# Edge counts of a graph layer: the first tile without registers, its tables built earlier, low halves of three weight pages moved

## What is computed

```python
e = leaky_relu(s_src[src] + s_dst[dst], 0.2)
emax = segment_max(e, dst, num_segments=n)
ee = exp(e - emax[dst])
denom = segment_sum(ee, dst, num_segments=n)
alpha = ee / denom[dst]
out = segment_sum(alpha[:, :, None] * h[src], dst, num_segments=n)
```

## Time and profile before

| | us |
|---|---|
| median of three runs | 1904.43 (1903.36 to 1904.77) |
| the profiled execution, own time | 1903.6 |
| its span, first to last instruction | 1901.9 |
| TensorE busy | 1851.5 |
| VectorE busy | 1296.5 |
| ScalarE busy | 654.5 |
| GpSimd busy | 558.1 |

### The profile page before, as it was taken

The page is one execution under the profiler, slowest core; times in us unless marked ns, Lnnn a source line. Parts: engine busy times, 40 slices in busy tenths (PEclk is TensorE's granted clock), DMA queues, the critical chain, the costliest instruction groups (busy, mean ns, idle before and its releaser), DMA issues.

```text
span 1901.9 us, 28584 instructions
## 1 busy us (share of the span) xinstructions
PE 1851.5 (97%) x10824; PEld 1758.4 (92%) x10824; DVE 1296.5 (68%) x2242; ACT 654.5 (34%) x1243; POOL 558.1 (29%) x441
## 2 busy tenths in 40 slices
PE   6999999999899999999999999999999999999998
PEld 4678999999899999989999999999999999999998
DVE  7987579998894323878796654454558966465548
ACT  6534238887884411225211111111341111211113
POOL 1000001210001132214355654444024455455420
PEclk9999999999999999999999999999999999999999
DMA  5433302122244210033311111111240111111314
GB/s 166 123 117 103 104 14 59 44 58 60 70 142 140 67 50 1 26 98 106 97 41 34 34 50 34 51 48 56 80 139 26 34 50 35 50 34 34 112 47 125
DMA packets 83133, 131.17 MB, mean 69 GB/s; under 512 B 7462, under 2 KB 53320, under 8 KB 82990
## 3 DMA queue, kind: packets, MB, share of 16 engines
q1 hardware_dynamic: 78430, 115.97, 20.8%
q10 hardware_dynamic: 4560, 13.31, 2.3%
HBM read 101.06 MB, written 28.20 MB: 68 GB/s over the span
## 4 chain that ended last, share of the span: by engine, by line
PE 86%; DVE 5%; ACT 5%; issue 3%; ACTq 0%; SPq 0%; DVEq 0%; DMA 0%
PE pb L809 20%; PE pa L809 17%; PE pb L1304 11%; PE pb L1284 9%; PE pa L870 5%; PE pb L1314 5%; PE pb L947 3%; PE pa L1029 3%; PE pb L1190 3%; PE pa L983 2%; PE pb L1029 2%; ACT sm L1787 1%; PE pb L817 1%; PE pb L1065 1%; ACT o1h L1813 1%
## 5 line engine op out<-in xcount | busy, mean ns | idle before, releaser
L809 PE MATMUL pa<-dw_hi,hh 128*125 128x384 f32 x608 | 156.8, 339 | 1.7 <-issue 1.1
L809 PE MATMUL pa<-dw_hi,hl 128*125 128x384 f32 x608 | 156.0, 338 | 0.0
L809 PE MATMUL pa<-dw_lo,hh 128*125 128x384 f32 x608 | 155.6, 337 | 0.0
L2713 DVE TENSOR_TENSOR hl<-tr,hh 128x448 fp32r<-128x448 f32 x144 | 152.1, 1056 | 5.0
L2711 DVE CAST hh<-tr 128x448 fp32r<-128x448 f32 x144 | 78.7, 546 | 88.2 <-ACT tr L2047 83.0
L2081 ACT ACTIVATE cp<-pb 128x448 f32<-128x448 f32 x32 | 17.4, 544 | 323.1 <-PE pb L1304 316.4
L2047 ACT ACTIVATE tr<-pb,V 128x448 f32<-128x448 f32 (+1 forms) x96 | 57.1, 597 | 198.7 <-PE pb L1284 142.1
L1492 POOL CAST dw_hi<-raw 128x768 fp32r<-128x768 f32 x48 | 49.2, 1025 | 230.7 <-PE pa L809 228.5
L870 PE MATMUL pa<-S1h,D1h 125*125 125x418 bf16 x510 | 103.4, 356 | 8.1 <-DVE S1h L2207 8.1
L809 PEld LDWEIGHTS pa<-dw_hi,hh 128*125 128x125 f32 x608 | 108.8, 185 | 2.2 <-issue 1.3
L809 PEld LDWEIGHTS pa<-dw_lo,hh 128*125 128x125 f32 x608 | 109.6, 185 | 0.0
(11 more groups left out here) (470 smaller groups left out, 5134.7 us busy)
## 6 DMA issues: line engine op xcount, KB each, us to landing
raw<-in_L_mix_fc_w SPq DMA_DIRECT2D x48, 384.0 KB, 3.4
raw<-in_L_ffn_w SPq DMA_DIRECT2D x47, 384.0 KB, 3.4
md<-md_d SPq DMA_DIRECT2D x11, 546.9 KB
md_d<-mds SPq DMA_DIRECT2D x10, 546.9 KB
raw<-in_L_mix_qkv_w SPq DMA_DIRECT2D x24, 192.0 KB, 4.2
md<-md_d ACTq DMA_DIRECT2D x8, 546.9 KB
TOK<-in_x SPq DMA_DIRECT2D x10, 336.0 KB
xn_d<-TOK SPq DMA_DIRECT2D x10, 336.0 KB
```

The lines of the kernel that those rows point to most:

```text
L809: last = nc.tensor.matmul(slot[:, c, :], x_[:, cols], w_[:, c * HD2:(c + 1) * HD2], start=(k == 0 and n == 0), stop=(k == len(blocks) - 1 ...
L2713: v.tensor_tensor(hb_lo[b][:, o:o + w], z, hb_hi[b][:, o:o + w].bitcast(fp32), ALU.subtract).then_inc(sem("h_lo"), 1)
```

## The change

The start of the first tile's rows is written as the constant 0, so that VectorE needs no register for its 16 fixed products and can begin once the limits `bc` are formed; `bc[0, 3]` is set to 85 by a `memset`, with one more chained wait. The copy to `bnd` moves behind the fourth product's tables, and the register for the loop count is loaded behind the sixteenth. On TensorE the three transposes of the small vectors move behind the sixth product, and the register loads for tile 0 and 1 behind the sixteenth. The low parts of the Wu pages, which stood as 0 and 1 before the loop and 2 behind tile 0, now stand as 0 behind tile 0, 1 behind tile 1 and 2 behind tile 2. Nothing changes on ScalarE, GpSimd and SP.

```diff
--- before.py
+++ after.py
@@ -242,7 +242,7 @@
                 kept[name] = (kind, before)
                 before += n
 
-        follow("pe_once", ("e_bb", 1), ("e_tr", 1), ("v_tr", 1), ("e_row", 1), ("tb0", 1), ("tb1", 1), ("r_log", 1), ("r_gb", 1))
+        follow("pe_once", ("e_bb", 1), ("e_tr", 1), ("e_row", 1), ("v_tr", 1), ("tb0", 1), ("tb1", 1), ("r_log", 1), ("r_gb", 1))
         follow("pe_rows", ("wt_mm", NT), ("g_mm", 2 * NT), ("kv_mm", 2 * NT), ("qg_mm", QJOBS), ("pj_mm", NT))
         follow("pe_side", ("c0_mm", 1), ("ssb_mm", 2 * NT), ("ssb2_mm", NT), ("xm_tr", NT), ("l_tr", NT), ("y_tr", NT))
         follow("pe_sums", ("e_acc", NT), ("at_o", STEPS), ("kvp", 2 * NT))
@@ -832,11 +832,13 @@
                     last = nc.tensor.transpose(pb[0:TP, 1, (2 * v + half) * EW:(2 * v + half) * EW + NEP],
                                                RM["ef"][:, v, half * TP:(half + 1) * TP], ident[0:NEP, 0:NEP])
             last.then_inc(sem("e_tr"), 1)
-            pe.wait_ge(*at("v_in", 16 * (len(VROWS) + len(VROWS2) + 1)))
-            vst = RM["t0_0"]
-            nc.tensor.transpose(pb[:, 0, 0:NV1], vst[0:NV1, 0:P], ident[0:NV1, 0:NV1])
-            nc.tensor.transpose(pb[:, 0, P:P + NV2], vst[0:NV2, P:2 * P], ident[0:NV2, 0:NV2])
-            nc.tensor.transpose(pb[0:C2, 0, 2 * P:2 * P + 2], vst[0:2, 2 * P:2 * P + C2], ident[0:2, 0:2]).then_inc(sem("v_tr"), 1)
+            def vector_transposes():
+                pe.wait_ge(*at("v_in", 16 * (len(VROWS) + len(VROWS2) + 1)))
+                vst = RM["t0_0"]
+                nc.tensor.transpose(pb[:, 0, 0:NV1], vst[0:NV1, 0:P], ident[0:NV1, 0:NV1])
+                nc.tensor.transpose(pb[:, 0, P:P + NV2], vst[0:NV2, P:2 * P], ident[0:NV2, 0:NV2])
+                nc.tensor.transpose(pb[0:C2, 0, 2 * P:2 * P + 2], vst[0:2, 2 * P:2 * P + C2], ident[0:2, 0:2]).then_inc(sem("v_tr"), 1)
+
             pe.wait_ge(*at("e_bc", 1))
             nc.tensor.matmul(pb[0:1, 3, 0:NT], RM["bc"][:, 0:1], ident[0:NT, 0:NT], start=True, stop=True)
             nc.tensor.matmul(pb[0:1, 3, 16:16 + NT], RM["bc"][:, 2:3], ident[0:NT, 0:NT], start=True, stop=True)
@@ -861,7 +863,7 @@
                     pe.wait_ge(*at("v_cp", 1))
                 if t >= 2:
                     pe.wait_ge(*at("e_sb", t - 1 if t <= XFIRST else t))
-                if t < XFIRST:
+                if 0 < t < XFIRST:
                     turns_of(t + 1)
                     turns_before(t + 1)
 
@@ -874,6 +876,13 @@
                 for n in range(2 * FIXED):
                     pe.wait_ge(*at(f"oh{n % RING}", fixed_use(turns, t, n)))
                     edge_products(n % RING, n == 0)
+                    if t == 0 and n == 5:
+                        vector_transposes()
+                if t == 0:
+                    pe.wait_ge(*at("bnd", 1))
+                    turns_of(0)
+                    turns_of(1)
+                    turns_before(1)
                 with pe.Fori(0, turns[t][0]) as p:
                     for q in range(2):
                         pe.wait_ge(*at(f"oh{q}", fixed_use(turns, t, 2 * FIXED + q) + p))
@@ -908,9 +917,7 @@
                     last = nc.tensor.matmul(pa[0:TP, 2 + c, 0:HD2], ones[:, 0:TP], RE["c0w"][:, c * HD2:(c + 1) * HD2], start=True, stop=True)
                 last.then_inc(sem("c0_mm"), 1)
 
-            pe.wait_ge(*at("bnd", 1))
             pe.wait_ge(*at("c_const", 3))
-            turns_of(0)
             for t in range(NT):
                 edge_counts(t)
                 for u in x_tiles(t):
@@ -2171,16 +2178,19 @@
             ch.link(v.tensor_scalar(bb[:, 0, :], pb[0:NT, 2, 0:NEP], bc[:, 7:8], None, ALU.is_lt))
             ch.link(v.scalar_tensor_tensor(out=bb[:, 1, :], in0=pb[0:NT, 2, P:P + NEP], scalar=bc[:, 6:7],
                                            in1=bb[:, 0, :], op0=ALU.is_ge, op1=ALU.mult))
-            v.tensor_tensor_reduce(out=bb[:, 3, :], in0=bb[:, 1, :], in1=ix[:, 1, :], scale=1.0, scalar=1.0,
-                                   op0=ALU.mult, op1=ALU.max, accum_out=bc[:, 3:4])
+            ch.link(v.tensor_tensor_reduce(out=bb[:, 3, :], in0=bb[:, 1, :], in1=ix[:, 1, :], scale=1.0, scalar=1.0,
+                                           op0=ALU.mult, op1=ALU.max, accum_out=bc[:, 3:4]))
+            v.memset(bc[0:1, 3:4], float(NEP))
             ch.link(v.tensor_tensor_reduce(out=bb[:, 2, :], in0=bb[:, 1, :], in1=ix[:, 0, :], scale=1.0, scalar=0.0,
                                            op0=ALU.mult, op1=ALU.max, accum_out=bc[:, 4:5]))
             ch.link(v.tensor_scalar(bc[:, 0:1], bc[:, 3:4], -1.0, float(NEP), ALU.mult, ALU.add))
             ch.link(v.tensor_scalar(bc[:, 1:2], bc[:, 4:5], bc[:, 0:1], FIXED + 1.0, ALU.subtract, ALU.max))
             v.tensor_scalar(bc[:, 2:3], bc[:, 1:2], -float(FIXED), None, ALU.add).then_inc(sem("e_bc"), 1)
-            dve.wait_ge(*at("e_row", 1))
-            v.tensor_copy(bnd[:].rearrange("p (a b) -> p a b", b=NT),
-                          pb[0:1, 3, 0:48].rearrange("p (a b) -> p a b", b=16)[:, :, 0:NT]).then_inc(sem("bnd"), 1)
+            def row_bounds():
+
+                dve.wait_ge(*at("e_row", 1))
+                v.tensor_copy(bnd[:].rearrange("p (a b) -> p a b", b=NT),
+                              pb[0:1, 3, 0:48].rearrange("p (a b) -> p a b", b=16)[:, :, 0:NT]).then_inc(sem("bnd"), 1)
 
 
             edges = {}
@@ -2188,7 +2198,7 @@
             def edges_of(t):
 
                 if t < NT:
-                    edges[t] = [dve.value_load(bnd[0:1, t:t + 1], min_val=0, max_val=NEP - 1)]
+                    edges[t] = [dve.value_load(bnd[0:1, t:t + 1], min_val=0, max_val=NEP - 1) if t else 0]
 
             def turns_of(t):
 
@@ -2210,6 +2220,11 @@
                 for n in range(2 * FIXED):
                     dve.wait_ge(*at(f"oh_used{n % RING}", fixed_use(edges, t, n)))
                     one_hot(n % RING, edges[t][0] + n // 2, n % 2)
+                    if t == 0 and n == 3:
+                        row_bounds()
+                if t == 0:
+                    dve.wait_ge(*at("bnd", 1))
+                    turns_of(0)
                 with dve.Fori(0, edges[t][1]) as p:
                     for q in range(2):
                         dve.wait_ge(*at(f"oh_used{q}", fixed_use(edges, t, 2 * FIXED + q) + p))
@@ -2258,20 +2273,16 @@
                 v.scalar_tensor_tensor(out=pair[1][:], in0=raw[i % NRAW][:], scalar=gain, in1=pair[0][:].bitcast(fp32),
                                        op0=ALU.mult, op1=ALU.subtract).then_inc(sem("bw_split"), 1)
 
-            for k in range(2):
-                page_low(PG_WU + k, wu[k])
-            dve.wait_ge(*at("bnd", 1))
             dve.wait_ge(*at("e_ec", 1))
             dve.wait_ge(*at("c_const", 3))
             edges_of(0)
-            turns_of(0)
             for t in range(NT):
                 one_hots(t)
                 if t >= XFIRST + 2:
                     graph_rows(t - XFIRST - 2)
                 if t == XFIRST + 1:
                     x_low(0)
-                for k in {0: (2,), 3: (3, 4, 5)}.get(t, ()):
+                for k in {0: (0,), 1: (1,), 2: (2,), 3: (3, 4, 5)}.get(t, ()):
                     page_low(PG_WU + k, wu[k])
                 edges_of(t + 1)
                 if ln_tiles(t):
```

## The result

The changed kernel took 1922.18 us (median of 5, 1920.56 to 1923.0), the kernel before beside it 1903.36 (1902.35 to 1904.77). The ratio is 1.0097, with a 95% interval of 1.0086 to 1.0108: slower by 18.8 us in medians. The profiled execution has a span of 1920.5 us against 1901.9, so 18.6 more. The forecast was 1920.5, with a range of 1917 to 1924, so the median lies 1.7 us above it.

What follows compares the result with a forecast made beforehand. TensorE, busy for 97% of the span, was taken as the bound, so only delays ahead of 57 us count. Tile 3's shift of +16.8 us, start gain included, on 1903.6 gave 1920.4, forecast as 1920.5, range 1917 to 1924.

Steps and rivals of the forecast that it cites:

- The mechanism: Wu pages: page 2's late low part delays page 5's load, holding ScalarE's copy of tile 1 by 16.6 us, then tile 3.
- Rival 1: Tile 3 on TensorE: the restart is not slow, so +14.5 us and 1918.1 in all; chance 0.17.
- Rival 2: Whole kernel: not slower, only the start's gain of 1.9 us is left, 1901.7; chance 0.05.
- rival 3: SP's queue: bunched stores, or VectorE's wait for the logarithm, cost tile 3 or 4 another 3.7 us, 1924; chance 0.08.
- the stores behind SP's queue: SP behind page 5's load: tile 0's table store at some 58, there by 62, needed after 72; costed at nothing.
- Rival 4: Start: bounds' chain 0.3, transposes 0.7, loads 0.5 more; +1.5 on the forecast, 1922; counted within the forecast's 0.70.
- end of tile 0: Tile 0 on TensorE: moves from 27.0 to 25.1 us, by 1.9, after 0.8 for the register loads.
- copy of tile 1: ScalarE's copy of tile 1's counts, behind page 5's high part: starts at 57.25 instead of 40.69 us, later by 16.6.
- `X_lo` behind tile 3's tables: VectorE's low part following tile 3's tables: these end at 84.0 us against 67.2, a shift of +16.8.
- tile 2's length: VectorE's tables for tile 2: begin at 39.0 for 40.93 and end at 51.9 for 53.84 us.
- The slow restart of tile 3: TensorE after 19 us with almost nothing to do: tile 3 starts at the 1.2 GHz level, +16.8 instead of +14.5 us.
- The small terms: Start: memset and chained wait 0.1 us taken; bounds' copy 0.2 and transposes 0.7 hidden; register loads 1.1 to 1.5.

Runs made afterwards that it cites:

- Experiment 3: The kernel before with only the low parts of Wu pages 0, 1 and 2 moved as in the change; 1922.58 us, ratio 1.0094.
- experiment 1: The changed kernel with the low parts of Wu pages 0, 1 and 2 all behind tile 0; 1902.58 us, ratio 0.9989 against the kernel before.
- experiment 2: The changed kernel with page 5's high part behind ScalarE's logarithm of tile 2, not ahead of tile 1's copy; 1904.71 us, ratio 1.0002 against before.
- experiment 4: The changed kernel with 24 unread matmuls of 418 columns on TensorE ahead of tile 3; 1920.65 us, ratio 1.0082 against the kernel before.
- 7, start only: The changed kernel with the low parts where they were before, so only the new start remains; 1905.29 us, ratio 1.0008 against the kernel before.
- 8, page 5 half late: The changed kernel with low parts 0 and 1 behind tile 0 and 2 behind tile 1; 1903.96 us, ratio 0.9994 against the kernel before.
- experiment 6: As experiment 1, with two of TensorE's three register loads moved behind tile 0; 1903.42 us, ratio 0.9993 against the kernel before.
- experiment 5: As experiment 6, with unread filler matmuls on TensorE ahead of tiles 0 and 2; 1901.38 us, ratio 0.9981 against the kernel before.

## Why the prediction was right, and where it was off

**The mechanism** was right in each link: page 2's low part late, so page 5's load late, so ScalarE held ahead of tile 1's copy, so TensorE held ahead of tile 3. Experiment 3 shows that the low parts are enough for the loss, 1 that taking them back is enough to undo it, and 2 that it is ScalarE's place in line by which the late page costs all but some 2 us. Rival 1 (a restart that isn't slow) falls with the clock of 0.50 and experiment 4. Rival 2 (only the gain is left) falls with the result, and rival 3 (SP's queue adds more) with the trace: no other wait came on top. But its premise was nearer than I had it. I costed the stores behind SP's queue at nothing, with the table's store issued at 58 and there by 62; in experiment 2 it was issued at 58.4 and there only at 66.4. The 72.2 at which ScalarE's copy of tile 2 comes in the changed kernel still covered that. Rival 4 (less gain at the start) named 1922, the number that came nearest, but none of its three terms is in the trace: tile 0 ended at 24.98, ahead of the 25.1 forecast.

**The terms of the sum**, predicted and read:

| step | predicted | read |
|---|---|---|
| first product of tile 0 | 11.3 | 11.27 |
| end of tile 0 | 25.1 | 24.98 |
| root done on ScalarE | 36.7 | 36.57 |
| tile 2's first table | 39.0 | 38.92 |
| end of page 2's low part | 52.7 | 54.26 |
| page 5 landed, from issue | 3.7 | 3.62 |
| copy of tile 1 | 57.25 | 58.66 |
| tile 3 starts | 72.1 | 73.49 |
| `X_lo` behind tile 3's tables | 84.0 | 85.58 |
| whole, against the execution before | +16.8 | +18.6 |

Up to tile 2's start everything is within 0.15 us. For tile 0's end that is luck: in experiment 4, with the same instructions up to there, it came at 26.22. **The step that was mis-sized is tile 2's length**: "Tile 2's tables begin at 39.0 for 40.93 and end at 51.9". I took its 12.9 us as fixed and the gap ahead of it as harmless, since it had been so in the one trace I had. The runs show that it isn't fixed. The table has the time from tile 2's first product to the end of its last matmul, with the idle time ahead of it and the granted clock from 42 to 46 us:

| run | idle before | tile 2 took | clock |
|---|---|---|---|
| before | 2.71 | 13.1 | 1.00 |
| after | 3.06 | 14.7 | 0.57 |
| 2, high part later | 3.06 | 14.7 | 0.56 |
| 7, start only | 3.07 | 14.7 | 0.50 |
| 8, page 5 half late | 3.06 | 13.6 | 0.84 |
| 4, busy ahead of tile 3 | 3.07 | 13.7 | 0.69 |
| 3, low parts only | 2.81 | 13.7 | 0.61 |
| 1, all behind tile 0 | 2.41 | 13.7 | 0.69 |
| 6, loads behind | 1.94 | 13.1 | 1.00 |
| 5, fillers | none | 13.1 | 1.00 |

With a slow level tile 2 took 0.5 to 1.6 us more than the 13.1 of the fast ones. In the changed kernel that is 1.55 us, and since the low part of page 2 now stands right behind tile 2's tables, all of it goes into the stall. In this execution it is the missing part of the sum: 16.8 + 1.5 = 18.3 of the 18.6. The rest is small differences along the way. In experiment 4, up to tile 3 the same kernel, 1.2 us of the delay lay in tile 0 and 0.6 in tile 2, so the size belongs to the slow starts together and its split to the execution.

**The slow restart of tile 3**, on which I chose +16.8 over +14.5, was right: clock 0.50 from 73 to 78, and 2.5 us by experiment 4, against the 2.3 that lay between my two sums. The Trainium skill ("TensorE: Matmul & The Clock Gate", Part 1) has an idle array fall back to half rate, and the rows behind this long wait agree. I had used tile 2's fast start after 2.7 us as a reason for doubt, and did not ask whether tile 2 itself would start fast in the next execution. The rows of the shorter gaps show both.

**The small terms** held: the memset ahead of the bounds cost nothing that can be read, as the step behind it ended at 9.80 as before; the copy of the bounds and the transposes (0.36 us on TensorE) are not seen in tile 0's end; the register loads held TensorE for 1.45 us.

## What to carry to other kernels

Where a buffer ring hands a free slot from one engine to a DMA and from there to a second engine, an instruction moved later on the first one moves everything that stands behind the load's consumer, in that consumer's order. Its own cost (0.95 us here) says nothing of that. For each moved release, write down the load that it gates, who takes that load in and what that engine has in line behind it, and compare with the room there was; here 8 us of room against 27 us of delay. And where a stage's first products follow a gap of 2 to 3 us, the sum should carry the slow start as a spread, here 0.5 to 1.6 us, since the same kernel may show it in one execution and not in another.

## What the runs showed of the hardware

Gaps of 2 to 3 us on TensorE were followed by a slow start in some executions and not in others, and the length alone doesn't decide which. Ahead of tile 2, 2.71 us left the clock at 1.00 in the kernel before, and behind 2.41 us it was 0.69 in experiment 1. Ahead of tile 1, 2.19 us was followed by 0.58 (27 to 30 us) in experiment 5 and by 1.00 in experiment 6. The stop of 2.02 us near 990 us was followed by 1.00 in the kernel before and in experiment 1, and by 0.50 in experiment 6. The five gaps of 3.06 or 3.07 us ahead of tile 2 were all followed by a slow start. With 12 fillers in the gap (5) it stayed at 1.00. One such start cost 0.5 to 1.6 us here, so which gap is harmless can't be told from one trace, and a shift of 1.5 us that first appears late in a trace says nothing about a change at its beginning.

At the start of the program the granted clock is no guide. Its column reads 1.00 up to 20 us in all ten kernels, while tile 0's first matmuls take 555 to 562 ns and, in the kernel before, start 347 ns apart (15 in 5.20 us). And 9 filler matmuls (18 in the rows) with 4.5 us of busy time did not bring it to the faster level: tile 0's first 18 matmuls took 6.31 us with them and between 4.81 and 6.30 in the six other kernels that start at 11.2 to 11.3. Why, was not settled. That spread of 1.5 us, by the same instructions, also bounds what one trace can tell of a change of a microsecond at the start.
